# Four attention and feed-forward layers on one core: biases and weight slabs issued a slot sooner, and six instead of four last units turned by TensorE

## The reference, cut to what matters

```python
x = x + _L0_xattn_ref(_layernorm(x), ctx, mask, q, k, v, o, q_norm, k_norm)   # 32 heads, 64 keys per batch
x = x + _L0_ffn_ref(_layernorm(x), weight, bias, gate_w, ...)                 # binary weights, 8 routed scales
x = x + _L1_xattn_ref(...); x = x + _L1_ffn_ref(...)
x = x + _L2_xattn_ref(_layernorm(x), ctx, mask, fside, Wq, Wk, Wv, Wo)        # 32 heads, a bias per head
x = x + _L2_ffn_ref(...)
x = x + _L3_xattn_ref(_layernorm(x), ctx, Wq, Wk, Wv, Wo)                     # keys are context and latents
x = x + _L3_ffn_ref(...)
```

## Time and profile before

| | us |
|---|---|
| median of 3 runs | 2300.43 (2299.38 to 2303.16) |
| the profiled execution | 2308.12 |
| its span in the trace | 2306.3 |
| TensorE busy | 2123.8 (92%) |
| VectorE busy | 1324.1 (57%) |
| ScalarE busy | 1161.9 (50%) |
| GpSimd busy | 539.6 (23%) |

### The profile page before, as it was taken

One profiled execution on the slowest core, in us unless ns is written; L12 is line 12 of the kernel. 1 busy time (PEld: TensorE's weight loads), 2 busy tenths in 40 slices (PEclk: granted clock), 3 DMA queues, 4 the chain that ended last, 5 costly groups with the idle time before them and its releaser, 6 DMA issues.

```text
span 2306.3 us, 40169 instructions
## 1 busy us (share of the span) xinstructions
PE 2123.8 (92%) x13684; PEld 1155.4 (50%) x13684; DVE 1324.1 (57%) x2695; ACT 1161.9 (50%) x3004; POOL 539.6 (23%) x936
## 2 busy tenths in 40 slices
PE   4899898999899889999999999998869799999998
PEld 2555555655554434555455455555424355555554
DVE  5566666666651465665566556655552456666654
ACT  4666566666412235555555455543232466666651
POOL 3332332323310312222222122212210122222221
PEclk9999999999989899999999999999889999999999
DMA  3111212211121112332323223212210132333221
GB/s 124 56 45 57 64 38 61 55 46 38 32 110 48 38 61 75 72 90 72 90 72 76 79 72 90 72 35 58 92 37 1 32 79 74 91 77 77 60 56 37
DMA packets 186725, 146.23 MB, mean 63 GB/s; under 512 B 163434, under 2 KB 171882, under 8 KB 176546
## 3 DMA queue, kind: packets, MB, share of 16 engines
q1 hardware_dynamic: 186082, 143.71, 22.8%
q10 hardware_dynamic: 448, 0.03, 0.0%
HBM read 102.29 MB, written 2.10 MB: 45 GB/s over the span
## 4 chain that ended last, share of the span: by engine, by line
PE 64%; DVE 14%; ACT 12%; issue 7%; DMA 1%; POOL 1%; SPq 0%; DVEq 0%; ACTq 0%; POOLq 0%
PE bank L84 18%; PE bank L85 17%; PE bank L86 17%; ACT m_E L460 3%; PE bank L1842 3%; PE bank L1488 2%; DVE m_Sm L886 2%; ACT m_arena L338 2%; ACT m_arena L439 2%; DVE m_x L937 2%; PE bank L1388 1%; DVE m_A L931 1%; DVE m_arena L732 1%; DVE m_nmax L903 1%; ACT m_arena L430 1%
## 5 line engine op out<-in xcount | busy, mean ns | idle before, releaser
L832 DVE TENSOR_TENSOR m_arena<-bank,m_arena 128x512 f16<-128x512 f32 x320 | 221.3, 691 | 486.3 <-ACT m_arena L439 486.0
L84 PE MATMUL bank<-m_input_parts,m_arena 128*128 128x512 f16 x1088 | 420.2, 386 | 8.8 <-DVE m_arena L832 2.6
L85 PE MATMUL bank<-m_input_parts,m_arena 128*128 128x512 f16 x1088 | 419.8, 386 | 0.0
L86 PE MATMUL bank<-m_input_parts,m_arena 128*128 128x512 f16 x1088 | 419.3, 385 | 0.0
L949 POOL TENSOR_TENSOR m_E<-m_E,m_rinv 128x512 f32<-128x512 f32 (+1 forms) x192 | 173.7, 905 | 795.0 <-DVE m_rinv L917 795.0
L460 ACT ACTIVATE m_E<-m_Sm,m_nmax 128x64 f32<-128x64 f32 (+1 forms) x512 | 185.4, 363 | 295.2 <-DVE m_nmax L903 148.4
L439 ACT ACTIVATE m_arena<-bank 128x512 f16<-128x512 f32 x320 | 189.3, 592 | 241.8 <-PE bank L86 241.4
L84 PE MATMUL bank<-m_wo_t,m_A 128*128 128x512 f16 x768 | 294.5, 383 | 0.0
L85 PE MATMUL bank<-m_wo_t,m_A 128*128 128x512 f16 x768 | 294.0, 383 | 0.0
L86 PE MATMUL bank<-m_wo_t,m_A 128*128 128x512 f16 x768 | 293.7, 382 | 0.0
L84 PE MATMUL bank<-m_arena,m_input_parts 128*128 128x128 f16 (+1 forms) x768 | 185.6, 273 | 7.2 <-DVE m_arena L837 6.3
(11 more groups left out here) (281 smaller groups left out, 4166.3 us busy)
## 6 DMA issues: line engine op xcount, KB each, us to landing
m_raw<-a_q SPq DMA_DIRECT2D x24, 1024.0 KB, 4.9
m_raw<-a_o SPq DMA_DIRECT2D x24, 1024.0 KB, 5.0
m_raw<-a_k SPq DMA_DIRECT2D x9, 1024.0 KB, 4.9
m_raw<-a_v SPq DMA_DIRECT2D x9, 1024.0 KB, 5.3
m_bias_in<-bias SPq DMA_DIRECT2D x64, 128.0 KB, 2.3
m_arena<-f_w SPq DMA_DIRECT2D x3, 1024.0 KB, 7.6
m_PT<-m_split SPq DMA_TRANSPOSE x180, 3.0
m_x<-x SPq DMA_DIRECT2D x2, 1024.0 KB, 7.1
```

The source lines that it names most:

```text
L84: pe.matmul(out, lhs[0], rhs[0], start=first, stop=False)
L85: pe.matmul(out, lhs[0], rhs[1], start=False, stop=False)
L86: return pe.matmul(out, lhs[1], rhs[0], start=False, stop=last)
L832: ins = dve.tensor_tensor(self.dest(name, part, 1), self.shaped(name, bank[m % 2][:, :]), self.dest(name, part, 0), ALU.subtract)
```

## The change

1. `MOVED` becomes `UNITS - 6`: units 58 and 59 of the attentions of layers 0, 2 and 3 are turned by TensorE like 60 to 63.
2. SP issues each bias of layer 2 one slot earlier (`slot - 3` for `slot - 4`).
3. SP issues the weight slabs one slot earlier (two slots for none; the table is `ahead`). The slab of the output matrix for the next period now stands in slot 7 of the period before, ahead of that slot's transposing transfer; the first one is issued by itself at t = 0.
4. `load_tail` stands in slot 0 of period 8 instead of slot 1.

The waits of each transfer on its semaphores are the same in number.

```diff
--- before.py
+++ after.py
@@ -97,7 +97,7 @@
 
     CHAIN = {"dve": {0: 0, 2: 16, 3: 8}, "pool": {0: 17, 2: 13, 3: 10}}
 
-    MOVED = UNITS - 4
+    MOVED = UNITS - 6
 
     def __init__(self, k, layer, dram, before, before_count):
         self.k, self.layer, self.dram = k, layer, dram
@@ -310,20 +310,26 @@
                                    k.split[:, b % 2].rearrange("p i n -> p (i n)")[:, 0:n])\
                 .then_inc((s["pt0"], s["pt1"])[b % 2].sem, 16)
 
+        ahead = {0: {0: 1, 3: 2, 4: 3}, 2: {1: 1, 3: 2, 5: 3}, 3: {1: 1}}[self.layer]
+
+        def slab(t, n, g):
+            self.load(sp, self.kinds[n], g, self.NP + n + self.NK * parity(t), at(t, self.NK, self.NP + n - 1))
+
         def emit(t, events):
             kinds = {7: 1, 8: 0}.get(t, self.NK) if isinstance(t, int) else self.NK
+            if isinstance(t, int) and t == 0:
+                slab(t, 0, 0)
             for slot in range(8):
-                if self.layer == 2 and (not isinstance(t, int) or 0 <= 8 * t + slot - 4 < UNITS):
-                    bias(t, slot - 4)
-                n = {0: 0, 1: 1, 4: 2, 5: 3}.get(slot, 4) if self.layer == 0 else 4 if slot % 2 else slot // 2
+                if self.layer == 2 and (not isinstance(t, int) or 0 <= 8 * t + slot - 3 < UNITS):
+                    bias(t, slot - 3)
+                n = ahead.get(slot, kinds)
                 if n < kinds:
-                    kind = self.kinds[n]
-                    g = at(t, 1, 0 if kind == "o" else 1)
-                    self.load(sp, kind, g, self.NP + self.NK * 0 + n + (self.NK * parity(t)),
-                         at(t, self.NK, self.NP + n - 1))
+                    slab(t, n, at(t, 1, 0 if self.kinds[n] == "o" else 1))
+                if slot == 7 and (not isinstance(t, int) or t < 7):
+                    self.load(sp, "o", at(t, 1, 1), self.NP + self.NK * (1 - parity(t)), at(t, self.NK, self.NP + self.NK - 1))
                 if self.by_dma(t, slot - 5):
                     turn(t, slot - 5)
-                if isinstance(t, int) and t == 8 and slot == 1:
+                if isinstance(t, int) and t == 8 and slot == 0:
                     self.next.load_tail(sp)
 
         self.periods(sp, emit)
```

## The result

| | before | after |
|---|---|---|
| median, us | 2299.90 (4 runs, 2299.29 to 2303.16) | 2278.64 (4 runs, 2277.09 to 2284.27) |
| profiled execution | 2308.12 | 2279.01 |
| span in its trace | 2306.3 | 2277.2 |

The ratio of after to before is 0.9909, 95% interval 0.9884 to 0.9933: 21.3 us faster. The changed kernel was timed twice more, beside runs of the kernel before: 2276.7 beside 2303.4 (ratio 0.9888, 0.9869 to 0.9908) and 2282.3 beside 2303.6 (0.9911, 0.9888 to 0.9933).

A forecast was written before the change was run, and what follows sets the result against it. It took TensorE to bound the attention loops, so sooner DMAs gain only where somebody waits for their landing. 16.1 - 3.1 + 1.0 = 14.0 us gained, giving 2286.4 us against the median; range 2281 to 2296.

The forecast's parts named there:

- The tails: Ends of attention layers 0, 2, 3: earlier tail loads end the first logit group's DMA stall, gaining 16.1 us together.
- the circle: Tail chain between residual additions, statistics through halves: 5.99, 8.65, 6.40 us without a stall in layers 0, 2, 3.
- The rival that the circle takes more: Tail slots run longer than read, or slow clock persists: half the gain, 7 us, lost; 2293 us; 17%.
- The rival that the load is as late as before: In the tails, misc_read or the landing, not queue place, holds the logits; only cost left: 2302.5 us; 6%.
- The rival that TensorE is the bound: In the tails TensorE's full loss comes back: 19.0 us gained in all, 2281.4 us; 9%.
- The two more units on TensorE: Units 58 and 59 in the three tails: extra transposes and halves lose 3.1 us, bounds 0 and 6.
- Biases: Layer 2's biases a slot sooner: GpSimd's waits, 22.3 us, delay nothing VectorE needs at once; gain 0, bounds 0 and 1.
- Slabs: Slabs a slot sooner: only ScalarE's wait in layer 3's first period goes; gain 1.0 us, bounds 0 and 1.3.
- Slower, transfers behind slabs: Layer 3's transposing transfers, behind slabs, land 1.4 us late for 15 slabs: 21 us lost, 2307 us; 5%.

The follow-up runs named there:

- b_again: The kernel before, unchanged, run again for a second profiled execution: 2301.58 us.
- e_slabs: The kernel before with all weight slabs alone issued by the new table, tails and biases as before: 2293.18 us, ratio to before 0.9964.
- e_o_only: The kernel before with the output-matrix slab a_o alone moved to slot 7 of the period ahead: 2292.66 us, ratio to before 0.9953.
- e_o_top: The changed kernel with slab a_o put back to slot 0 of the period that uses it: 2290.41 us, ratio to before 0.9947.
- e_o_behind: The changed kernel with slab a_o still in slot 7, but behind that slot's transposing transfer: 2287.08 us, ratio to before 0.9927.
- a_again: The changed kernel, unchanged, timed again with a second profiled execution: 2276.70 us.
- third_look: The changed kernel, unchanged, as reference for a later set of runs: 2282.28 us, ratio to before 0.9911.
- e_tail: The kernel before with the tails alone changed (last six units turned by TensorE, load_tail in slot 0): 2290.77 us, ratio to before 0.9962.
- e_no_tail: The changed kernel with the tails alone undone (four units turned by TensorE, load_tail in slot 1): 2292.90 us, ratio to before 0.9948.
- e_bias_late: The changed kernel with layer 2's biases alone issued a slot later again, as before: 2280.92 us, ratio to before 0.9904.

## Why the prediction was wrong

**The tails: right.** Forecast 5.32, 4.77 and 6.00 us; the additions of unit 58 moved by 5.34, 4.79 and 6.01 from the first trace of before to that of after. That this agrees to 0.02 us says only that the circle of slot 1 is now as long as that of slot 2, since the stall was read from the same trace; in b_again the excess is 5.5, 4.9 and 5.1. The rival that the circle takes more (2293) fell: its lengths are those forecast to 0.1 us. The rival that the load is as late as before fell with the waits. The rival that TensorE is the bound (2281.4) fell too: the waits gone are the circle's, not TensorE's full loss, though the total came out closer to its number. A right number would have had a wrong reason there.

**The two more units on TensorE: right.** Forecast 3.1 us; from trace to trace 0.34 and 0.27 in layer 0, 0.44 and 0.60 in layer 2, 0.43 and 0.60 in layer 3, 2.7 in all. The 60 transposes took 10.7 us, four in some 0.7 us, as in the earlier trace rows.

**Biases: right**, nothing, though all 22.3 us of GpSimd's waits for them went away.

**Slabs: this step failed.** I wrote "ScalarE waited for a slab once", 1.0 us, "bounds 0 and 1.3", "Elsewhere nobody waits: 0". The 1.0 was fair for what it priced: the first five additions of layer 3 take 28.3 to 28.8 us in five of the six profiles with a_o late, and 27.5 in all others. But b_again has 27.5 too, with a_o late, so this wait doesn't come in every execution. The term priced only those who wait for a slab to land, and not what stands still at a turn of the loop while the slab is in flight. That term measured 8.3 us for all slabs (e_slabs, by its ratio), and for a_o's place alone 10.8 (e_o_only, by its ratio), 13.7 (e_o_top) and 10.4 (e_o_behind). The upper bound of 1.3 had no row under it for this; the rows were there, in the chain of waits, marked "issue". The prediction wrote of "59 us in small pieces" and never took them apart; it read the loops by TensorE's waits. The sentence "the loops are bound by TensorE, and a DMA that is issued sooner can gain only where somebody waits for its landing" is what failed, as a rule.

With 16.1 - 3.1 + 1.0 and some 10 us for a_o's place the sum is 24 us, against 21.3, 26.7 and 21.3 measured. **Slower, transfers behind slabs: fell.** e_o_behind, with the slab behind the transfer, is the slower one.

**What stays open.** The turns explain 8.6 us between the groups, and moving a_o gave 10 to 14. Ahead of the attentions of layers 2 and 3 the groups' means differ by another 2.2 us, but there the executions of one kernel differ by up to 4 us, in steps of slow clock (below), and no experiment took that apart. One at a time on the kernel before, the parts add up to 14.0 us (8.7 + 8.3 - 3.0), which is less than the 21 to 27 of the whole change; taken out of the changed kernel, tails and a_o's place give 24. The intervals are too wide to say whether the parts help each other. Layer 3's loop shows nothing, with the same slab in flight; its trace has no packets of the kind "instruction" to hold up, but why it needs none was not tried. That these packets were slow, as the mechanism has it, is inferred: the profile lists how many there were, not how long each took.

## What to carry to other kernels

Look at a large transfer not only from the side of who waits for it, but also for what the engines must do while it is in flight; at a loop's branch that is, by all that these runs show, the fetch of their own instructions. Where the chain of waits or the list of waits shows "issue" of 1 to 4 us behind a branch, look at which DMA is in flight there and whether there are packets of the kind "instruction", and let the large transfer land before the branch or start behind it. Time the same kernel's profile twice before a difference of 2 us at one place is explained.

## What the runs showed of the hardware

**Behind a loop's branch** VectorE was without work, at the first turn of layer 0, 3.4 to 3.9 us in six of the seven profiles with 1 MB in flight, 1.0 in the seventh, where a_o came later, and 0.8 to 1.9 us in the other eleven. At the second turn the two groups overlap: 0.9 to 4.2 and 0.8 to 2.6 us. So the wait is never quite gone. A 1 MB transfer in flight where no instruction packets were moved, at layer 3's turns, cost nothing.

**The kernel's times scatter** by more than the four first runs said: 2292.9 to 2308.8 for the kernel before over all sets, 2272.7 to 2285.8 for the changed one. Steps of 2 to 4 us that come in one execution and not in the next make that up. Some are turns, and some are of the clock. One of those, in the stage between the attentions, windows of 2 us of b_again (columns as above):

```profile
790.00:792.00 2.00, 0.62 (x4) 0.38 (x4) 1.90 (x5) 0.60 (x1) 1.83 (x3) 1.00 0.00 0
792.00:794.00 2.00, 1.79 (x6) 1.30 (x7) 1.56 (x2) 0.60 (x1) 2.00 (x3) 0.52 0.00 0
794.00:796.00 2.00, 2.00 (x4) 0.81 (x3) 0.03 (x1) 0.00 (x0) 2.00 (x2) 0.62 0.00 0
796.00:798.00 2.00, 2.00 (x8) 0.97 (x7) 0.06 (x1) 0.00 (x0) 0.37 (x1) 1.00 0.00 0
```

and the same work in the kernel after:

```profile
786.00:788.00 2.00, 0.41 (x4) 0.34 (x4) 1.51 (x4) 0.60 (x1) 1.83 (x3) 1.00 0.00 0
788.00:790.00 2.00, 2.00 (x8) 1.04 (x7) 1.48 (x1) 0.60 (x1) 2.00 (x2) 1.00 0.00 0
790.00:792.00 2.00, 2.00 (x9) 0.94 (x7) 0.21 (x1) 0.00 (x0) 1.86 (x2) 1.00 0.00 0
```

Before it TensorE was busy 0.62 of 2 us in the one and 0.41 in the other. In the first the granted clock then is 0.52 and 0.62 for 4 us, which means 3.4 us at 1.2 GHz and 1.7 us of work lost; in the second it stays at 2.4 GHz. From layer 0's last addition to layer 2's first, read in windows of 2 us, the lower clock costs 15.3, 17.1, 18.8 or 20.5 us in the 18 profiles, steps of 1.7 again: 15.3 in after and a_again, 17.1 in third_look, which is the same kernel, and 18.8 in before and b_again. That accounts for the 3.3 us at the start of layer 2 in the first pair of traces. The parts of the change don't sort it: e_tail and e_slabs have 15.3 and 15.4, e_no_tail 18.8 and e_bias_late 20.5. So idle time costs clock in one execution and not in another, and a forecast can only give it a share.
